# Mixture-of-experts layer on one core: the small rests of the experts' token lists put in pairs into four double tiles, and token gathers issued one tile further ahead

## The reference

```python
gate_probs = jax.nn.softmax(gate_logits, axis=-1)
top_v, top_i = jax.lax.top_k(gate_probs, TOP_K)          # TOP_K = 2, E = 8
onehot = jax.nn.one_hot(top_i, E, dtype=x.dtype)
comb_w = jnp.einsum('bsk,bske->bse', top_v, onehot)
out = jnp.zeros_like(x)
for e in range(E):
    h = jax.nn.silu(jnp.einsum('bsh,hf->bsf', x, w1[e]) + b1[e])   # 256 -> 1024
    y = jnp.einsum('bsf,fh->bsh', h, w2[e]) + b2[e]                # 1024 -> 256
    out = out + y * comb_w[..., e:e + 1]
```

## Time and profile before

| what | value |
|---|---|
| median of three runs | 332.39 us (331.66 to 332.83) |
| the profiled execution, its own time | 334.24 us |
| its span, first to last instruction | 332.4 us |
| mean granted clock | 0.99 of full speed |
| busy: PE, DVE, ACT, POOL | 308.5, 246.0, 195.4, 198.7 us |
| expert tiles worked on (scatters) | 37 |

### The profile page before, as it was taken

One profiled execution on the slowest core, in us unless ns is written; L12 is line 12 of the kernel. 1 busy time (PEld: TensorE's weight loads), 2 busy tenths in 40 slices (PEclk: granted clock), 3 DMA queues, 4 the chain that ended last, 5 costly groups with the idle time before them and its releaser, 6 DMA issues.

```text
span 332.4 us, 10153 instructions
## 1 busy us (share of the span) xinstructions
PE 308.5 (93%) x3309; PEld 252.8 (76%) x3309; DVE 246.0 (74%) x581; ACT 195.4 (59%) x551; POOL 198.7 (60%) x223
## 2 busy tenths in 40 slices
PE   8699989999998868999999999999999999999990
PEld 7458879888887668788787877878787787878760
DVE  5659998889988964876868777777778687556551
ACT  2442467676564555766666767677576766544530
POOL 3367899997864042175666656576747656566423
PEclk9999999999999998999999999999999999999998
DMA  7799999999999942244546473645536454655222
GB/s 249 232 347 419 399 421 410 410 410 405 343 383 385 330 179 51 50 66 83 63 83 84 64 92 57 97 62 88 80 68 73 74 89 67 90 81 84 36 34 33
DMA packets 50549, 58.76 MB, mean 177 GB/s; under 512 B 23880, under 2 KB 44576, under 8 KB 48320
## 3 DMA queue, kind: packets, MB, share of 16 engines
q0 software_dynamic: 9408, 26.63, 33.3%
q1 hardware_dynamic: 35776, 28.09, 27.6%
q10 hardware_dynamic: 5312, 3.37, 3.3%
HBM read 43.32 MB, written 10.16 MB: 161 GB/s over the span
## 4 chain that ended last, share of the span: by engine, by line
PE 58%; POOL 13%; issue 11%; DVE 9%; ACT 5%; ACTq 1%; DMA 1%; DVEq 1%; POOLq 0%
PE ps L1187 24%; PE ps L1200 14%; PE ps L1201 7%; PE ps L1002 3%; POOL w_parts L512 3%; POOL sel L512 2%; POOL sel L544 2%; PE ps L915 2%; PE ps L1206 2%; PE ps L1011 2%; ACT w_parts L854 2%; DVE sel L1601 2%; POOL w_parts L544 1%; DVE sel L1603 1%; ACT sel L892 1%
## 5 line engine op out<-in xcount | busy, mean ns | idle before, releaser
L1187 PEld LDWEIGHTS ps<-sel,w_parts 128*128 x1776 | 121.0, 99 | 33.9 <-issue 2.7
L1187 PE MATMUL ps<-sel,w_parts 128*128 128x128 f16 x1776 | 141.1, 221 | 1.6 <-DVE sel L1603 1.6
L632 POOL DMA_INDIRECT out<-sel x37 | 60.1, 1626 | 76.3 <-ACT sel L878 56.3
L892 ACT ACTIVATE sel<-ps,b1T 128x128 f32<-128x128 f32 x296 | 83.1, 369 | 22.3 <-PE ps L1187 20.3
L1200 PE MATMUL ps<-w_parts,sel 128*128 x259 | 95.9, 379 | 0.3 <-DVE sel L1603 0.3
L1201 PE MATMUL ps<-w_parts,sel 128*128 x259 | 70.6, 273 | 0.0
L1588 DVE SCALAR_TENSOR_TENSOR w_parts<-w_parts (+1 forms) x32 | 39.2, 1228 | 32.3 <-ACT w_parts L854 23.7
L1603 DVE SCALAR_TENSOR_TENSOR sel<-sel 128x512 f16<-128x512 f32 x74 | 51.2, 692 | 2.5
L624 POOL DMA_INDIRECT sel<-tokens_split,sel x37 | 42.9, 1159 | 16.6 <-DVE sel L1570 9.8
L1601 DVE TENSOR_SCALAR sel<-sel 128x512 f16<-128x512 f32 x74 | 32.1, 434 | 17.5 <-ACT sel L892 15.9
L878 ACT ACTIVATE sel<-xn,sel 128x256 f32<-128x256 f32 x37 | 18.8, 508 | 42.5 <-DVE xn L1643 36.4
(11 more groups left out here) (228 smaller groups left out, 425.7 us busy)
## 6 DMA issues: line engine op xcount, KB each, us to landing
w_parts<-in_L_ffn_w SPq DMA_DIRECT2D x16, 1024.0 KB, 12.3
out<-xs SPq DMA_DIRECT2D x16, 128.0 KB
tokens_split<-xsplit ACTq DMA_DIRECT2D x13, 128.0 KB, 5.5
xs<-in_x ACTq DMA_DIRECT2D x2, 512.0 KB, 6.9
xs<-in_x SPq DMA_DIRECT2D x2, 512.0 KB, 8.1
near_rows<-w_parts SPq DMA_DIRECT2D x4, 256.0 KB, 8.9
xs<-in_L_ffn_b SPq DMA_DIRECT2D x1, 1024.0 KB, 5.5
sel<-tokens_split,sel POOLq DMA_INDIRECT x37
```

The costliest lines, as they stand in the source:

```text
L632: pool.indirect_dma_start(out_rows, bass.IndirectOffsetOnAxis(slot_row[:, at(q - 1)], 0), y_sb[(k + 3) % 4], None, compute_op=ALU.add).the ...
L892: act.activation(h32[n][:, c * P:c * P + P], ps_h[n][:, c * P:c * P + P], ACT.Silu, bias=biases[:, c:c + 1], scale=1.0 / (X_SCALE * W_SCALE))\
L1187: mm = pe.matmul(ps_h[n][:, c * P:c * P + P], w, xx, start=(i == 0), stop=(i == len(products) - 1))
```

## The change

A tile is now full for the rows of one expert up to its last 128, and a rest of at most 64 rows goes into half of a *double tile* with the rest of another expert; a rest above 64 makes one more full tile. Every expert has one half, also one with no rows in it. There are at most `N_FULL` = 35 full tiles, of which `SURE` = 28 always run, and `PAIRS` = 4 double tiles. `JOBS` puts a double tile behind full tiles 6, 12, 18 and 24, so as jobs 7, 14, 21 and 28 of 39. The halves of a double tile belong to the experts of ranks 2n and 2n + 1 in number of full tiles.

In a double tile every up product is made twice, with each expert's weights over 64 of the 128 token columns: 96 products of 64 columns. The down-projection has the weights as stationary side and gives the result turned (features by rows): per chunk 4 products of 2 x 64 columns and 4 of 64. DVE adds the bias `b2T` per side (`pair_out`), TensorE turns the sum back with two float32 transposes (`pair_rows`, behind chunk 3 of the step after the down-projection), ACT scales each half from PSUM, and POOL scatters the two halves by two DMAs of 64 rows; the second stands in the next step, behind that step's gather. ACT makes 16 Silu of 64 columns. Two experts' numbers are loaded from `order_i` where one was.

For full tiles the products are unchanged. POOL gathers tile q + 5 in step q, and the first four gathers stand ahead of the wait for `RT_LIST`. The table needs a few more links (below, and seven on DVE in step 2, `half_list`). Two waits of TensorE are now counted by expert (`weights_ready`).

The diff, cut to its core:

```diff
-    NT = T * TOP_K + E - 1
-    FULL = T * TOP_K
+    HALF = P // 2
+    N_FULL = (B * S * TOP_K + E * (HALF - 1)) // P
+    SURE = (B * S * TOP_K - E * HALF) // P
+    PAIRS = E // 2
+    NL = N_FULL + PAIRS
+    JOBS = []
+    for f in range(N_FULL):
+        JOBS.append((False, f))
+        if f % 6 == 0 and 0 < f < SURE:
+            JOBS.append((True, f // 6 - 1))
+    NT, ALWAYS = len(JOBS), SURE + PAIRS
...
+            def tokens_gathered(q):
+
+                if q == JOBS.index((True, 0)):
+                    pool.wait_ge(s["rt"], RT_HALF)
+                wait(pool, "slot_w_ok", q - 3)
+                pool.indirect_dma_start(xg[q % 4], None, xd,
+                                        bass.IndirectOffsetOnAxis(slot_row[:, at(list_column(q))], 0))\
+                    .then_inc(s[f"gathered{q % 4}"], 16)
+
...
+            for q in range(4):
+                tokens_gathered(q)
+            pool.wait_ge(s["rt"], RT_LIST)
+            tiles = tile_count(pool)
...
+                        if is_pair(q + 1):
+                            e = [expert_in_pair(pool, q + 1, i) for i in range(2)]
+                            turned(pool, q + 1)
+                            for i in range(2):
+                                product = pool.tensor_tensor(slot_w[:, at(weight_column(q + 1, i))],
+                                                             xg[(k + 1) % 4][:, bass.ds(e[i] + D, 1)],
+                                                             valid[:, at(column)], ALU.mult)
+                            product.then_inc(s["slot_w_ok"], 1)
...
+                if live(5):
+                    with filled(pool, tiles, q + 5):
+                        tokens_gathered(q + 5)
+                if live(-2) and is_pair(q - 2):
+                    scattered_to(q - 2, slice(HALF, P), slot_odd[:, at(JOBS[q - 2][1])], scatters_ahead(q - 2) + 1)
...
+                        for i in range(2):
+                            rows = rows_of_half(i)
+                            scaled = act.activation(y_sb[t % 4][rows, :], ps_rows[rows, :], ACT.Copy,
+                                                    scale=slot_w[rows, at(weight_column(t, i))])
+                        scaled.then_inc(s["y_ok"], 1)
...
+                            for i, own in enumerate(biases):
+                                cols = slice(c * P + i * wide, c * P + i * wide + wide)
+                                silu = act.activation(h32[n][:, cols], ps_h[n][:, cols], ACT.Silu, bias=own[:, c:c + 1],
+                                                      scale=1.0 / (X_SCALE * W_SCALE))
+                            silu.then_inc(s["silu_ok"], 1)
...
+            def up_chunk(q, c, spots):
+
+                n, wide = q % 2, HALF if is_pair(q) else P
+                for side, own in enumerate(spots):
+                    to, products = slice(c * P + side * wide, c * P + side * wide + wide), []
+                    for kc in range(KC):
+                        hi, lo = (weights_at(own[2 * kc + part], P) for part in range(2))
+                        products += [(hi, kc), (hi, KC + kc), (lo, kc)]
+                    for i, (w, a) in enumerate(products):
+                        mm = pe.matmul(ps_h[n][:, to], w, xT[n][:, a, side * wide:side * wide + wide], start=(i == 0),
+                                       stop=(i == len(products) - 1))
...
+            def pair_down_chunk(q, c, spots):
+
+                n = q % 2
+                for side, own in enumerate(spots):
+                    rows = slice(c * P + side * HALF, c * P + side * HALF + HALF)
+                    for j in range(KC):
+                        sides = ps_y[n][:, j * D:j * D + D].rearrange("p (a r) -> p a r", a=2)
+                        sides = sides[:, :, side * HALF:side * HALF + HALF]
+                        pe.matmul(sides, weights_at(own[2 * j], P), h_both[n][:, :, rows],
+                                  start=(c == 0 and j == 0 and side == 0), stop=False)
+                        mm = pe.matmul(sides[:, 0, :], weights_at(own[2 * j + 1], P), h_hi[n][:, rows], start=False,
+                                       stop=(c == FC - 1 and j == KC - 1 and side == 1))
...
+            def pair_rows(q):
+
+                m = JOBS[q][1]
+                pe.wait_ge(s["y_sum_ok"], q + 1)
+                if m > 0:
+                    pe.wait_ge(s["y_ok"], JOBS.index((True, m - 1)) + 1)
+                for j in range(KC):
+                    mm = pe.transpose(ps_rows[:, j * P:j * P + P], xn[:, q % 2, j * P:j * P + P], ident[:, :])
+                mm.then_inc(s["rows_ps"], 1)
...
+                        if c == 3 and live(-2) and is_pair(q - 2):
+                            pair_rows(q - 2)
...
+                        pe.reg_load(pair_of, order_i[0:1, 2 * n:2 * n + 3])
...
+            link(v.tensor_tensor(r_end[:, :], r_first[:, :], r_tf[:, :], ALU.add))
+            v.scalar_tensor_tensor(out=r_hop[:, :], in0=r_rank[:, :], scalar=0.5, in1=r_end[:, :],
+                                   op0=ALU.mult, op1=ALU.subtract)
             dve.wait_ge(s["rt_ps"], 2)
-            link(v.scalar_tensor_tensor(out=r_from[:, :, :], in0=spread_mid(r_first[:, :], T), scalar=float(P),
-                                        in1=ps_base.rearrange("p (t e) -> p t e", e=E), op0=ALU.mult, op1=ALU.add))
+            link(v.scalar_tensor_tensor(out=r_over[:, :, :], in0=spread_mid(r_tf[:, :], T), scalar=float(P), in1=base,
+                                        op0=ALU.mult, op1=ALU.is_le))
+            v.scalar_tensor_tensor(out=r_from[:, :, :], in0=spread_mid(r_first[:, :], T), scalar=float(P), in1=base,
+                                   op0=ALU.mult, op1=ALU.add)
+            link(v.scalar_tensor_tensor(out=r_over[:, :, :], in0=spread_mid(r_hop[:, :], T), scalar=float(N_FULL),
+                                        in1=r_over[:, :, :], op0=ALU.add, op1=ALU.mult))
+            link(v.scalar_tensor_tensor(out=r_from[:, :, :], in0=r_over[:, :, :], scalar=float(P), in1=r_from[:, :, :],
+                                        op0=ALU.mult, op1=ALU.add))
...
+            def pair_out(q, k, m):
+
+                sides = ps_y[m].rearrange("p (j a r) -> p a j r", j=KC, a=2)
+                own = [b2T[:, bass.ds(expert_in_pair(dve, q - 1, i) * KC, KC)].rearrange("p (j o) -> p j o", o=1)
+                       .to_broadcast([P, KC, HALF]) for i in range(2)]
+                dve.wait_ge(s["y_ps"], q)
+                wait(dve, "y_ok", q - 2)
+                for i in range(2):
+                    rows = rows_of_half(i)
+                    low = v.scalar_tensor_tensor(out=y_turn[m][:, :, rows], in0=own[i], scalar=H_SCALE * W_SCALE,
+                                                 in1=sides[:, 1, :, rows], op0=ALU.mult, op1=ALU.add)
+                low.then_inc(s["y_low_ok"], 1)
+                wait(dve, "y_low_ok", q)
+                v.tensor_tensor(y_turn[m], sides[:, 0, :, :], y_turn[m], ALU.add).then_inc(s["y_sum_ok"], 1)
```

356 lines of the change are left out of this document (222 added, 134 removed).

## The result

The changed kernel takes 327.09 us (median of 4 runs, 326.69 to 329.07) beside 332.61 us before (331.66 to 333.10): the ratio is 0.9857, with a 95% interval of 0.9828 to 0.9886. Run again later beside other kernels it took 328.05 us (6 runs), ratio 0.9861 [0.9823, 0.9898]. So it is faster by 1.4%, by the medians 5.5 and 4.3 us, where 12.0 were forecast; the time lies outside the range 317.5 to 326.0.

A forecast was written before the change was run, and what follows sets the result against it. PE was taken to be bound by columns, 5.28 us a step. From 334.24: -15.84 (three steps) + 0.5 (products) + 1.0 (transposes) + 1.2 (waits) + 1.1 (table) = 322.2, less 1.85: median 320.4 us, range 317.5 to 326.0.

The forecast's parts named there:

- 34 tiles: Expert stage: 30 full and 4 double tiles run in the place of 37 tiles, removing 3 x 5.28 = 15.84 us.
- The products of 64 columns: Double tile's products on PE: 28.4 ns each, by columns, +0.5 us for four double tiles, bounds nothing and +4.0.
- PE's sequencer: hidden: PE's instruction issue: a double tile's chunk takes 0.37 us, under its 0.67 on the array, so it costs nothing.
- The Silu: ACT, double tile: 16 of 64 columns for 8 of 128 add 0.8 to 2.1 us, hidden in ACT's idle time.
- The table: DVE's chain ahead of the slots: six operations for one, +1.1 us, bounds +0.8 and +1.5; all that follows is later.
- the wait of L1358: PE's first transpose waits for DVE's sum: 0.3 us for each of four double tiles, +1.2 us, bounds 0 and 1.5 each.
- the ring takes over: Rival, chance 0.07: waits at their upper bound, 4.8 us more, and double tiles' Silu not hidden, 4 us more: near 329.
- if PE waits over 1 us for a sum: Sign that the forecast is wrong: PE's wait for DVE's sum, forecast at 0.3 us a double tile, exceeds 1 us.
- the end (last sum to last scatter) stays: End of the program, POOL's scatters: the distance from last sum to last scatter does not change, 0 us.
- A gather now comes a step earlier, so this costs nothing: POOL: gathers queued behind late scatters are needed three steps later, so 0 us; without that cover 3 us each double tile.
- what a double tile costs PE besides: PE's added work for four double tiles: +0.5 us for shorter products and +1.0 us for two transposes each.
- The 1.85 us: The profiled execution before is 1.85 us above the median, so this is taken off 322.2 to give the median 320.4.

## Why the prediction was wrong

**Right:** 34 tiles. The products of 64 columns: 28.4 ns forecast, 28.9 measured, 5.43 and 5.40 us a step. "PE's sequencer: hidden": no wait of these steps on it. The Silu: 16 of 64 columns take 3.39 us for 2.16, +1.2 within +0.8 to +2.1. The full tiles at 5.28. The table: from L1496 (109.76) to L1501 (110.33) were 0.57 us, from L1666 (109.77) to L1681 (111.47) are 1.70, +1.13 for +1.1. The Trainium skill's rule for a weight load, "TensorE: Matmul & The Clock Gate", section "LDWEIGHTS (loading the stationary operand)" (an estimate of 107 ns for 128 columns), does not agree with this trace either: each of these products has its own load of 128 columns and starts 28.9 ns after the one before.

**Wrong, the wait of L1358.** "I take 0.3 us for each of the four, +1.2 us; the bounds are 0 and 1.5 each." It is 4.63 in three, over the upper bound in two. The mechanism was named (ACT scales a double tile's rows only after the transposes, and a ring hangs on that), and its price set too low in two places. The register loads were put at "some 0.4 us more" with two operations for one; DVE stands still for 0.95, 1.13 and 1.10 us for them alone, and moving them gave 3.7 us. And of the ring only the lateness was counted, some 0.8 us got back in seven steps, not that PE's own wait feeds it: with ACT's weights ahead of the scaled rows 3.3 us come back, 4.3 with the transposes later too. The rival "the ring takes over", near 329 with a chance of 0.07, had this mechanism; its Silu part (4 us) does not show, for with the short Silu the time is the changed kernel's. The prediction's own sign of being wrong, "if PE waits over 1 us for a sum", came three times.

**Wrong, "the end (last sum to last scatter) stays".** It is longer by 3.35 us. The prediction had the numbers: 4.03 us from scatter to scatter, "behind by some 3 us and catch up by 1.2 a step". It spent the catching up on the gathers and did not count it down to the end. There it can't catch up at all: from the last double tile's first half (296.85) to PE's last product are 16.6 us, and the five scatters of full tiles behind it alone take 20.4, as the kernel without second halves shows. So one distance more, 3.75, is paid nearly whole: the tail without the second halves is 3.75, with them 7.24. "A gather now comes a step earlier, so this costs nothing" is borne out on PE, where neither trace of the changed kernel shows a wait for tokens behind step 1; with the gathers a step later 1.5 to 2 us are lost.

**Too low, what a double tile costs PE besides.** 0.15 + 0.12 for the two steps, and 0.28 for the transposes with 0.1 to 0.2 around them, is some 0.7 for 0.37: +2.7 in all for +1.5. Transposes were costed by rows in which 14 run behind each other; alone they cost about 0.1 more.

**Wrong, the table: "all that follows, gathers and weights alike, is later by it".** DVE's chain and the first gather are 1.1 us later, as forecast, but the first up-projection is not (124.17 for 124.31), and step 1 ends 1.2 to 2.4 earlier in the two traces. 0.9 to 1.5 of that is the lower clock, which fell on the first up-projection before and does not now. The prediction named the clock there and took nothing. In other kernels with the same start step 1 ends as late as 138.73, so how much of this the median has is open.

So 4.6 us on PE and 3.4 in the tail too little, 2.3 to 3.5 at the start too much: 322.2 + 4.6 + 3.4 - 3.5 = 326.7 for the profiled execution (326.77). That the time is not further off is luck: the error at the start took back nearly half of the two others. The 1.85 us that the prediction took off from there to the median was a property of the traced execution before, not of the kernel: the changed kernel's traced executions, 326.77 and 327.98, stand near its medians, 327.09 and 328.05. Both traced executions before, 334.24 and 335.55, have the low clock in the up-projection and stand above its median; that the one makes the other is likely, but not shown.

## What to carry to other kernels

An instruction that waits for another engine should stand behind all that does not hang on it: here one swapped pair on ACT was worth 3.3 us on PE, where moving the wait itself by three chunks was worth 0.9 at most. Loads of registers are work, half a microsecond each here, wherever they stand between two operations of an engine that others wait for; put them where it waits anyway. And for a queue that needs most of a step per item, write down how far behind it is at each extra item, and carry the sum to the last one. And before a small edit is credited with a wait that shrank, look at the same wait in a kernel where nothing bears on it: here the three waits were 4.63 us in one trace and 2.9 in another.

## What the runs showed of the hardware

Two register loads on DVE, 314 and 190 ns each with their register instruction, cost 0.95 to 1.13 us of standing still in the first trace. An adding scatter of 64 rows holds the next for 3.6 to 3.8 us in the tail of the changed kernel, and one of 128 rows for 4.0 to 4.2: half the rows save a tenth. The Trainium skill has this as a fixed cost of some 2 us for a DMA, "DMA: Bandwidth & Descriptors", section "Latency and other measured facts"; the waits for a landing here, 2.1 to 2.6 us behind an issue of 1.4 to 1.8, agree with it. And with a longer chain ahead of the expert stage the stretch of TensorE's lower clock came earlier and no longer fell on the first up-projection: the two traces of the kernel before have a granted clock of 0.66 in 124 to 129 us, the 18 of kernels with the longer chain 1.00. What this is worth in the median no run shows.
